# A decoder layer on one core: a raw weight tile for each chunk of a pair, and two elementwise steps moved from VectorE to ScalarE

## What is computed

```python
xf = x.astype(jnp.float32) / 128.0
gate = jnp.einsum('bsh,ih->bsi', xf, w_gate)
up = jnp.einsum('bsh,ih->bsi', xf, w_up)
inter = jax.nn.silu(gate) * up
inter_q = jnp.trunc(jnp.clip(inter * 128.0, -128.0, 127.0)).astype(jnp.int8)
down = jnp.einsum('bsi,hi->bsh', inter_q.astype(jnp.float32), w_down)
out = jnp.trunc(jnp.clip(down * 128.0, -128.0, 127.0)).astype(jnp.int8)
```

## Time and profile before

| | |
|---|---|
| time, median of 3 runs | 1634.76 us (1633.28 to 1634.81) |
| the profiled execution, its own time | 1633.71 us |
| its span, first to last instruction | 1631.9 us |
| PE busy, of the span | 1552.8 us (95%) |
| DVE / POOL / ACT busy | 1000.0 / 689.2 / 664.3 us |
| mean granted TensorE clock | 0.989 |

### The profile page before, as it was taken

One profiled execution on the slowest core, in us unless ns is written; L12 is line 12 of the kernel. 1 busy time (PEld: TensorE's weight loads), 2 busy tenths in 40 slices (PEclk: granted clock), 3 DMA queues, 4 the chain that ended last, 5 costly groups with the idle time before them and its releaser, 6 DMA issues. The chain is left out here.

```text
span 1631.9 us, 22442 instructions
## 1 busy us (share of the span) xinstructions
PE 1552.8 (95%) x7792; PEld 1266.6 (78%) x7809; DVE 1000.0 (61%) x1575; ACT 664.3 (41%) x1329; POOL 689.2 (42%) x572
## 2 busy tenths in 40 slices
PE   7999999999999999999999999987799999999797
PEld 6888888888888888888888888864478777777543
DVE  4454454455445445435544544569878989899888
ACT  4423333152142333215214232544765564655574
POOL 3425244152342524325244252446676666666300
PEclk9999999999999999999999999998999999999999
DMA  7101100110110100011011010240113223222101
GB/s 289 47 26 65 40 27 26 51 39 13 64 39 26 64 31 34 26 51 39 13 64 39 26 65 27 73 183 1 40 39 104 97 96 103 100 95 100 52 39 66
DMA packets 28846, 98.51 MB, mean 60 GB/s; under 512 B 3584, under 2 KB 3968, under 8 KB 28800
## 3 DMA queue, kind: packets, MB, share of 16 engines
q1 hardware_dynamic: 28800, 97.93, 17.4%
HBM read 93.72 MB, written 4.19 MB: 60 GB/s over the span
## 5 line engine op out<-in xcount | busy, mean ns | idle before, releaser
L505 PE MATMUL ps<-xt_h,w_h 128*128 128x512 f32 x768 | 306.7, 399 | 8.4 <-DVE xt_l L1536 8.4
L1276 POOL TENSOR_TENSOR w_l<-w_raw,w_h 128x1024 fp32r<-128x1024 f32 x80 | 191.5, 2394 | 287.6 <-ACT w_h L846 287.6
L726 PE MATMUL ps<-xt_h,w_h 128*128 128x512 f32 x704 | 277.9, 395 | 25.5 <-ACT w_h L989 25.5
L507 PE MATMUL ps<-xt_h,w_l 128*128 128x512 f32 x768 | 300.4, 391 | 0.0
L506 PE MATMUL ps<-xt_l,w_h 128*128 128x512 f32 x768 | 300.0, 391 | 0.0
L727 PE MATMUL ps<-xt_l,w_h 128*128 128x512 f32 x704 | 275.2, 391 | 0.0
L1491 DVE TENSOR_TENSOR resid<-ps,resid 128x512 f32<-128x512 f32 x256 | 176.5, 690 | 140.3 <-PE ps L585 139.0
L1284 POOL TENSOR_TENSOR pm_l<-pt_l,upto 128x512 fp32r<-128x512 f32 x64 | 82.7, 1292 | 378.0 <-DVE pt_l L1479 375.7
L583 PE MATMUL ps<-w_h,o_h 128*128 128x512 f32 x512 | 204.4, 399 | 4.7 <-DVE resid L1491 3.3
L585 PE MATMUL ps<-w_h,o_l 128*128 128x512 f32 x512 | 201.2, 393 | 0.0
L584 PE MATMUL ps<-w_l,o_h 128*128 128x512 f32 x512 | 201.1, 393 | 0.0
(11 more groups left out here) (142 smaller groups left out, 2843.7 us busy)
## 6 DMA issues: line engine op xcount, KB each, us to landing
w_raw<-w_att SPq DMA_DIRECT2D x80, 512.0 KB, 3.3
w_raw<-w_gu SPq DMA_DIRECT2D x42, 512.0 KB, 3.3
d_raw<-w_down SPq DMA_DIRECT2D x22, 512.0 KB, 3.3
ctx_raw<-ctx_rows SPq DMA_DIRECT2D x8, 1024.0 KB, 6.3
resid<-x_cols SPq DMA_DIRECT2D x16, 256.0 KB, 6.2
resid<-x_rows SPq DMA_DIRECT2D x8, 512.0 KB, 7.4
out<-resid SPq DMA_DIRECT2D x8, 512.0 KB, 2.6
first_raw<-w_gu SPq DMA_DIRECT2D x1, 1024.0 KB, 5.0
```

The source lines that it names most:

```text
L505: pe.matmul(ps_out, wh, xt_h[:, c, rows], start=(c == 0), stop=False)
L507: last = pe.matmul(ps_out, wl, xt_h[:, c, rows], start=False, stop=(c == DC - 1))
L726: pe.matmul(dst, w, xt_h[:, c, rows], start=(c == 0), stop=False)
L1276: pool.tensor_tensor(w_l[:, w, :], w_raw[:, s % 2, :], w_h[:, w, :].bitcast(F32), ALU.subtract).then_inc(w_low, 1)
```

## The change

1. **Raw tiles.** Odd chunks are loaded into `resid[:, 0:2, :]`, the first two tiles of the residual rows. These rows are written out to a DRAM tensor `x2_rows` after the second layernorm and read back once all checks are counted; the first use of a residual row in the down stage waits for that (`rows_back`). `first_raw` is gone.
2. **ACT's and DVE's operations.** |v| becomes an ACT operation (`unit_size`, Abs). The cap at 127 leaves DVE: `inter` holds 127 - v as an unsigned byte, which ACT's store writes with Relu, bias 127 and scale -1, and `lhs` undoes with Identity, bias 127, scale -1.
3. **Order.** DVE takes the product of unit m first and then truncates unit m-1. ACT's order in a pair becomes: Silu 0, two counts of the even chunk, |v| 0, make `d_unit`, store of the previous unit 3; Silu 1, two makes of the even chunk, |v| 1, store 0, count of `d_raw`; Silu 2, two counts of the odd chunk, |v| 2, make `d_unit`, store 1; Silu 3, two makes of the odd chunk, |v| 3, store 2, count of `d_raw`. At the end DVE truncates unit 3 only after it has written `general`.
4. `u_val` and `u_size` get two buffers; `u_round` moves onto constants that are no longer used.

```diff
-        u_val = place("u_val", [P, HALF], F32, at_u + 4096)
-        u_size = place("u_size", [P, HALF], F32, at_u + 6144)
-        u_round = place("u_round", [P, HALF], F32, at_u + 8192)
-        u_again = place("u_again", [P, HALF], F32, at_u + 10240)
-        u_bound = place("u_bound", [P, 2, HALF], BF16, at_u + 12288)
+        u_val = place("u_val", [P, 2, HALF], F32, at_u + 4096)
+        u_size = place("u_size", [P, 2, HALF], F32, at_u + 8192)
+        u_again = place("u_again", [P, HALF], F32, at_u + 12288)
+        u_round = place("u_round", [P, HALF], F32, at_ident)
         d_raw = place("d_raw", [P, DM], F32, at_u + 14336)
         at_d = at_u + 14336 + 4 * DM
-        first_raw = place("first_raw", [P, 2, DM], F32, at_o)
         d_unit = place("d_unit", [P, FC, DM], BF16, at_d)
-        inter = place("inter", [P, FC, TOK], I8, max(at[0] - FC * TOK, at_d + 2 * FC * DM))
+        inter = place("inter", [P, FC, TOK], U8, max(at[0] - FC * TOK, at_d + 2 * FC * DM))
...
-            def load_units(c, i):
-                sp.dma_start(w_raw[:, i, :], w_gu[c, i]).then_inc(u_loaded[i], 16)
+            def load_units(c, k, i):
+                if k == 0:
+                    sp.dma_start(w_raw[:, i, :], w_gu[c, i]).then_inc(u_loaded[i], 16)
+                else:
+                    sp.dma_start(resid[:, i, :], w_gu[c, i]).then_inc(u1_loaded[i], 16)
...
             def load_pair(pair, first, last):
                 if not first:
-                    sp.wait_ge(u_counted, pair * U_PAIR + 2)
+                    sp.wait_ge(u_counted, pair * U_PAIR)
                 sp.dma_start(d_raw[:, :], w_down[pair * 2]).then_inc(ud_loaded, 16)
                 if not last:
                     for i in range(2):
-                        sp.wait_ge(u_counted, pair * U_PAIR + (3 + i))
-                        load_units(pair * 2 + 2, i)
-                sp.wait_ge(u_counted, pair * U_PAIR + 5)
+                        sp.wait_ge(u_counted, pair * U_PAIR + (1 + i))
+                        load_units(pair * 2 + 2, 0, i)
+                sp.wait_ge(u_counted, pair * U_PAIR + 3)
                 sp.dma_start(d_raw[:, :], w_down[pair * 2 + 1]).then_inc(ud_loaded, 16)
                 if not last:
                     for i in range(2):
-                        sp.wait_ge(u_counted, pair * U_PAIR + (6 + i))
-                        load_units(pair * 2 + 3, i)
+                        sp.wait_ge(u_counted, pair * U_PAIR + (4 + i))
+                        load_units(pair * 2 + 3, 1, i)
 
             for i in range(2):
                 sp.wait_ge(w_low, W_TILES - 1 + i)
-                load_units(0, i)
+                load_units(0, 0, i)
+            for i in range(2):
+                sp.wait_ge(ln_done[1], i + 1)
+                sp.dma_start(x2_rows[i], resid[:, i, :]).then_inc(rows_kept, 16)
+            sp.wait_ge(x2_turned, 2)
+            sp.wait_ge(rows_kept, 32)
+            for i in range(2):
+                load_units(1, 1, i)
             sp.wait_ge(wo_done, HKV * 2 * TILES * NH)
-            sp.dma_start(first_raw[:, :, :], w_gu[1].rearrange("i p n -> p i n")).then_inc(u1_loaded, 16)
             load_pair(0, True, False)
             with sp.Fori(1, PAIRS - 1) as pair:
                 load_pair(pair, False, False)
             load_pair(PAIRS - 1, False, True)
+            sp.wait_ge(u_counted, U_TILES)
+            for i in range(2):
+                sp.dma_start(resid[:, i, :], x2_rows[i]).then_inc(rows_back, 16)
...
+            def raw_of(k, i):
+
+                return w_raw[:, i, :] if k == 0 else resid[:, i, :]
+
             def make_gate_up(k, loaded):
 
                 for i in range(2):
-                    act.wait_ge(u_loaded[i], loaded)
-                    make_unit(w_h[:, 2 * k + i, :], w_raw[:, i, :], INV_G + i)
+                    act.wait_ge((u_loaded if k == 0 else u1_loaded)[i], loaded)
...
-            def count_gate_up(n, checked, raw=w_raw):
+            def count_gate_up(n, checked, k):
                 for i in range(2):
                     act.wait_ge(u_halved, (checked + i + 1) * 2)
-                    count(n + i, raw[:, i, :])
...
-            act.wait_ge(u1_loaded, 16)
-            for i in range(2):
-                make_unit(w_h[:, 2 + i, :], first_raw[:, i, :], INV_G + i)
+            make_gate_up(1, 16)
...
+            def unit_size(pair, m):
+
+                act.wait_ge(u_product, pair * 4 + (m + 1))
+                act.activation(u_size[:, m % 2, :], u_val[:, m % 2, :], ACT.Abs).then_inc(u_sized, 1)
+
             def unit_store(pair, m, by_batch):
+
                 i, b = unit_of(m, by_batch)
                 if by_batch and m == 0:
                     act.wait_ge(cross_done, TILES)
-                act.wait_ge(u_bounded, pair * 4 + (m + 1))
-                act.activation(inter[:, pair * 2 + i, b * SEQ:(b + 1) * SEQ], u_bound[:, m % 2, :], ACT.Copy).then_inc(u_stored, 1)
+                act.wait_ge(u_signed, pair * 4 + (m + 1))
+                act.activation(inter[:, pair * 2 + i, b * SEQ:(b + 1) * SEQ], u_size[:, m % 2, :], ACT.Relu,
+                               bias=param(TOP), scale=-1.0).then_inc(u_stored, 1)
...
                 unit_silu(pair, 0)
-                if first:
-                    count_gate_up(0, 0)
-                else:
-                    count_gate_up(second_chunk(pair), pair * 4 + 2)
+                count_gate_up(first_chunk(pair, first), pair * 4, 0)
+                unit_size(pair, 0)
+                down_made(0)
+                if not first:
                     unit_store(pair - 1, 3, False)
-                down_made(0)
 
                 unit_silu(pair, 1)
-                if first:
-                    count_gate_up(second_chunk(0), 2, first_raw)
-                elif not last:
+                if not first and not last:
                     next_made(0)
+                unit_size(pair, 1)
                 unit_store(pair, 0, first or last)
                 down_counted(first_down(pair), pair * 2 + 1)
 
                 unit_silu(pair, 2)
+                count_gate_up(second_chunk(pair), pair * 4 + 2, 1)
                 if first:
                     next_made(0)
-                elif not last:
-                    count_gate_up(next_chunk(pair), pair * 4 + 4)
+                unit_size(pair, 2)
+                down_made(1)
                 unit_store(pair, 1, first or last)
-                down_made(1)
                 if last:
                     stage(0)
                     down_counted(second_down(pair, True), 2 * PAIRS)
 
                 unit_silu(pair, 3)
-                if first:
-                    count_gate_up(next_chunk(0), 4)
-                elif not last:
+                if not last:
                     next_made(1)
+                unit_size(pair, 3)
                 unit_store(pair, 2, first or last)
                 if not last:
                     down_counted(second_down(pair, False), pair * 2 + 2)
-                if first:
-                    next_made(1)
...
-                act.activation(lhs[t % 2][:, :, :], inter[:, :, t * P:(t + 1) * P], ACT.Copy).then_inc(lhs_ready, 1)
+                act.activation(lhs[t % 2][:, :, :], inter[:, :, t * P:(t + 1) * P], ACT.Identity, bias=param(TOP),
+                               scale=-1.0).then_inc(lhs_ready, 1)
...
+            for k, raw in enumerate((w_raw, resid)):
+                for i in range(2):
+                    check_unit(k, i, 2 * k + i, 2 * k + i, raw)
...
-            def unit_truncate(pair, m, last):
+            def unit_product(pair, m, last):
                 n = pair * 4 + m
                 check = m in (1, 2 if last else 3)
                 dve.wait_ge(u_silu, n + 1)
+                dve.scalar_tensor_tensor(out=u_val[:, m % 2, :], in0=bank(U_BANK[m] + 1), scalar=param(SIZE_U),
+                                         in1=u_act[:, m % 2, :], op0=ALU.mult, op1=ALU.mult).then_inc(u_product, 1)
                 if check:
                     dve.wait_ge(u_made, (first_down(pair) if m == 1 else second_down(pair, last)) + 1)
-                dve.scalar_tensor_tensor(out=u_val[:, :], in0=bank(U_BANK[m] + 1), scalar=param(SIZE_U),
-                                         in1=u_act[:, m % 2, :], op0=ALU.mult, op1=ALU.mult).then_inc(u_product, 1)
-                if check:
-
                     dve.scalar_tensor_tensor(out=d_raw[:, :], in0=d_unit[:, pair * 2 + m // 2, :], scalar=param(SIZE_D),
                                              in1=d_raw[:, :], op0=ALU.mult, op1=ALU.not_equal).then_inc(ud_checked, 1)
-                dve.wait_ge(u_product, n + 1)
+
+            def unit_truncate(pair, m):
+
+                n = pair * 4 + m
+                sizes = u_size[:, m % 2, :]
 
                 def then(k, instruction):
                     instruction.then_inc(u_step, 1)
                     dve.wait_ge(u_step, n * U_STEPS + k)
 
-                then(1, size(u_size[:, :], u_val[:, :]))
```

(82 more changed lines are left out.)

10 lines of the change are left out of this document (6 added, 4 removed).

## The result

The changed kernel takes 1620.81 us (median of four runs, 1620.03 to 1621.55). The kernel before took 1634.64 beside it (1633.28 to 1634.81). The ratio is 0.9914, 95% interval 0.9902 to 0.9926: 13.8 us faster. The prediction said 1620.3. The profiled execution of the changed kernel took 1620.67 us.

The account below looks back on a forecast made before the run. POOL's check, with one pair of raw tiles for both chunks, bound the kernel at 31.7 us a pair. Start -7.0, nine pairs -17.3 and tail +9.8 gave -14.5 from 1634.76: 1620.3 us, range 1612 to 1630 (8 in 10).

Parts of the forecast that it names:

- Start: Up to Silu 1 of pair 1: ACT no longer waits for checks of the chunk just made; gain 7.0 us.
- The nine pairs: From Silu 1 of pair 1 to that of the last pair: 268.2 us instead of 285.5, gain 17.3.
- The ring: Middle pairs: Silu, product, truncation of the unit before, store, next Silu, without overlap; 29.8 us a pair.
- T: Truncation of one unit on DVE, four dependent operations: 4.15 us beside POOL's work, 2.6 with POOL done.
- |v| and the cap: Moved from DVE to ACT: |v| at price 0, the cap making each store 0.1 us longer.
- Parked rows: Two writes and two reads of 512 KB, 3.3 us each: taken at 0, with up to 3.3 us as bound.
- Tail: From the last pair's Silu 1 to the end of the second `lhs`: 32 us instead of 22.4, loss 9.8.
- TensorE's free rate: PE's pace without stalls in the middle: 29.3 us a pair, read over three chunks.
- the rival in which TensorE sets the pace: Middle pairs: T 4.0 or less, pair at PE's 29.3 us; 1616 us, or 1613 with a shorter tail; chance 0.18.
- The stalls at the end: PE idle about 6 us at unit 1 of the last pair and about 8 before the first `lhs`.
- Contention as today: Rival for the middle pairs: T = 4.4, pair 30.8 us, gain 5.3, 1629.5 us; chance 0.15.
- A ring slower than POOL's: Rival for the middle pairs: at T = 4.8 a pair takes 32.4 us, 9.1 us slower, 1644; chance 0.08.

Follow-up runs that it names:

- e1: Kernel before with only the raw tiles of odd chunks, parked rows and put-off counts added; truncation, |v| and cap as before: 1617.26 us.
- e3: Changed kernel with the cap at 127 taken on VectorE again, behind the sign and in front of the store: 1652.38 us.
- e4: Changed kernel with the stores of units 0, 1 and 3 put behind the next Silu, except in the last pair: 1614.2 us.
- e8: Changed kernel with |v| taken twice on ACT in each unit, the second time before VectorE may truncate: 1624.19 us.
- e10: Changed kernel without the two writes and two reads of the parked rows and the waits for them: 1620.77 us.
- e5: Changed kernel with only the last pair reordered: truncations not put off, stores before counts, first `lhs` made as early as the stores allow: 1614.71 us.
- e9: Changed kernel with each unit truncated right behind its own product, and |v| ahead of makes and counts on ACT: 1607.92 us.
- e7: Changed kernel with three of four stores behind next Silu, last pair reordered as in e5, and in pair 0 next chunk made before store and counts: 1603.14 us.

## Why the prediction was right, point by point

- **What bound the kernel.** POOL's turn with one pair of tiles: shown by e1, which leaves every operation of VectorE as it was and gains 17.4 us.
- **Start**, 7.0 foretold, 6.5 measured.
- **The nine pairs** came out at 268.4 for 268.2 partly by luck: the steady pair is 0.1 us shorter than foretold, 0.9 in nine, and the first of the nine took 30.82 us, 1.1 more than a steady one.
- **The ring.** T was put at 4.15 us; the truncation in the rows above takes 4.2 (1391.99 to 1396.23), in the next unit 4.1. With POOL idle the same four take 2.6 as foretold (1534.69 to 1537.29), the rounding 0.42 of it where 0.43 was put. The turns were put at 4.4 + T = 8.55 and 2.2 + T = 6.35, and are 8.60 and 6.25. The pair was 29.8 and is 29.70. That this is a ring and not load on an engine is shown from both sides: e3 makes it longer, e4 cuts it.
- **|v| and the cap.** |v| at no price holds in the middle (e8). The cap's 0.1 us on the store is there: 0.72 against 0.61. By e3 against the changed kernel ScalarE is the better place for the cap in this ring, by 32 us: the cap costs 1.40 us on VectorE beside POOL (0.43 where POOL leaves it alone) and 0.1 as a bias of a store that is made anyway. No table load came with it: the trace after has one of 1.28 us in front of the first Silu, as before.
- **Parked rows** at 0: shown by e10.
- **Tail**, 32 foretold, 32.7 measured. e5 shows that it is the order in the last pair that makes it.
- **The total** is nearer than its parts. All three terms came out on the side of less gain, -13.4 for -14.5, and the stretch behind them took 0.4 us more. The forecast missed by only 0.5 us because the profiled execution of the kernel before lay 1.05 us below its median and that of the changed kernel 0.14 below; that is luck. The prediction's arithmetic has small slips too: 32 less 22.4 is 9.6, not 9.8; the lower bound of a pair is 23.6, not 23.8; eight slow matmuls cost 1.6 us, not 1.7. None of them moves the forecast by more than 0.2 us.
- **TensorE's free rate** was put too high: 29.3 us a pair, read over three chunks, where 37 units give 29.04. So the ring is 0.66 above it, not 0.5, and the rival in which TensorE sets the pace would have been worth 9 x 0.26 = 2.3 us more than it said.
- **The stalls at the end** were put at 6 and 8 us and are 4.94 and 6.58.
- **The rivals.** TensorE at the pace: no, but e4 shows it as close as it was thought. Contention as today, 30.8 a pair: no, T is 4.2 and 4.1, not 4.4. By their means in 1260 to 1480 us its four operations add up to 4.10 us, without the gaps, and to 4.48 in the kernel before. That they shrink because two operations a unit are gone is not shown: in e3, with one more a unit than the changed kernel has, the four add up to 3.82. A ring slower than POOL's: no at T = 4.2; e3 is this rival come true (a pair of 32.4), one operation more a unit takes the kernel from 14 us faster to 18 slower. |v| on the ring, the rival of e8: no, with |v| taken twice the pair is 29.72.

What the prediction didn't ask was what each half would bring alone. Part of the answer was in its terms: the ring and the tail are both the second half's, and on top of the raw tiles that half costs 3.6 us (1617.26 to 1620.81). What its terms didn't show is that the loss is in the order alone. The moved operations by themselves are a gain, 9.3 us by e9 against e1.

## What to carry to other kernels

When a wait is removed, write down the next ring of dependent steps across the engines and compare its length with the busy engine's own time; here 29.70 against 29.04 us a pair. An operation put off by a unit costs nothing only while the engine that needs its result has something else to do; ahead of a store that stands before the next unit's start it closes a ring, and in the last round it is a tail (10 us here). Time the halves of a change apart: the full change gave 13.8 us, the raw tiles alone 17.4, and both halves with the order repaired 31.5 (e7).

## What the runs showed of the hardware

Beside GpSimd's work some of VectorE's operations took longer than alone, and these ended shortly after an instruction of POOL did. This is POOL beside the turn shown above:

```profile
1391.43 1.45 POOL L1407 TENSOR_SCALAR u_again<-w_h,prm 128x512 f32<-128x512 f32 x1 [4.05 <-ACT w_h L1004]
1392.97 1.61 POOL L1410 TENSOR_TENSOR w_raw<-u_again,w_raw 128x512 f32<-128x512 f32 x1
1394.78 0.91 POOL L1407 TENSOR_SCALAR u_again<-w_h,prm 128x512 f32<-128x512 f32 x1 [0.21 <-POOL w_raw L1410]
```

VectorE's L1752 began at 1393.45 and ended at 1395.12, 0.54 us after POOL's L1410 had at 1394.58; L1749 before it ended at 1393.42, again 0.54 us after POOL's L1407. All 29 L1749 in the trace from 1260 to 1480 us end so, 0.53 to 0.55 us after a L1407, and take 0.98 to 1.12. POOL's next one, 0.69 us when alone, took 0.91. So here a 128x512 operation with two inputs in SBUF costs VectorE 0.69 us alone and, by where POOL's stand, 0.98, 1.07 or 1.67 in the turn above, and the chain of rounding and three of them took 4.2 us there and 2.6 with POOL idle. The product, which reads PSUM and one tile of SBUF, took 0.75 in every row above. The cap in e3, with one input in SBUF, took 1.40 us (1413.09 to 1414.49) and ended 0.29 us after a L1410 of POOL's had at 1414.20; with POOL idle it took 0.43. What in the hardware holds VectorE up isn't shown.

It is not shown that fewer VectorE operations make POOL faster. In 1260 to 1480 us the mean of POOL's product fell from 1136 ns before to 930 after, but that of its subtraction rose from 1408 to 1529, so half a tile takes 2.54 and 2.46 us. In e3, with one VectorE operation more a unit than the changed kernel has, it takes 2.40.

After its two longest idle times in this stage TensorE came back at a lower clock. The windows, with the granted clock in the third column from the end, show 0.50 for the 4 us behind the stalls of 4.94 and 6.58:

```profile
1496.00:1500.00 4.00, 3.79 (x9) 3.02 (x10) 3.90 (x5) 0.68 (x2) 3.63 (x4) 0.50 0.02 4
...
1527.00:1531.00 4.00, 3.60 (x9) 1.48 (x11) 2.31 (x6) 2.19 (x4) 0.00 (x0) 0.50 0.48 164
```

Behind the stall of 2.42 us at 1222.61 the matmuls came 0.23 us apart at once, at a granted clock of 1.00 (1222.60 to 1226.00). Yet in e5 a stall of 2.44 us, at 1224.27, was followed by a granted clock of 0.50 (1224.20 to 1226.00), so the length of the idle time alone doesn't tell whether the clock drops. Not settled is why the end of the unchanged attention stage moves by up to 2.3 us from kernel to kernel; no run here was aimed at it. The table load in front of the first Silu isn't it: it takes 1.28 us in every run.
